# First-layer tables with column-tiled kernels and seven phase buffers, and a reordered feed-forward start and layer-1 projection

## What is computed

```python
# layer 0, attention a: the table. d is the distance, 1024 of them; 64 (batch, head) pairs
phase[h, m*8+w, d] = f1*d/S + f2*sqrt(d)/sqrt(S) + phi        # 3-term product, 16 heads x 128 kernels
feature = sin(2*pi * (phase - round(phase)))
n[b, h, d] = sum_mw gate_weight[b, h, m] * amp[h, m, w] * feature[h, mw, d]
hard = (n > 0); soft = sigmoid(6 * n)                         # straight-through step
bias[b, h, d] = (hard + (soft - hard)) * window[d]
table = (bias, exp(-bias))

# layer 0, mixture: 8 experts, top 2, and one shared expert
x += sum_e w_e(x) * W2_e relu(W1_e ln(x))**2  +  shared

# layer 1, attention a: latent = ln(x) W; q, k, v = latent W_u;
# rotary part r = (latent W_r) * cos + (latent W_r') * sin
```

## Time and profile before

| | us |
|---|---|
| median of 3 runs | 3451.47 |
| lowest and highest | 3448.38, 3469.87 |
| the profiled execution | 3457.46 |
| its span in the profile | 3455.7 |
| mean granted clock of TensorE in it | 0.933 of full |

### The profile page before, as it was taken

How to read it: one execution, slowest core, us unless ns; L and a number is a source line. 1 busy time by engine, 2 the same in 40 slices (tenths; PEclk the granted TensorE clock), 3 DMA queues, 4 the chain that set the end, 5 groups by cost and what they waited for, 6 DMA issues and landing times. The chain is left out here.

```text
span 3455.7 us, 67058 instructions
## 1 busy us (share of the span) xinstructions
PE 3053.0 (88%) x25109; PEld 1677.9 (49%) x25109; DVE 2373.2 (69%) x5084; ACT 1862.5 (54%) x3317; POOL 945.4 (27%) x655
## 2 busy tenths in 40 slices
PE   6778999958599999896799969998999999999899
PEld 3234444423276555573222237764455555555676
DVE  6578888848574554666799942235999999998321
ACT  5336666642264332463599924443666666666444
POOL 1029999971001322000000000001222223232100
PEclk8779999989798999897799969999999999999999
DMA  5212333210330000224322210017434344332000
GB/s 169 71 63 94 106 118 109 91 54 24 104 123 25 1 1 1 99 99 157 106 68 67 62 44 1 1 35 219 112 88 99 98 105 106 97 100 68 12 10 13
DMA packets 215138, 260.69 MB, mean 75 GB/s; under 512 B 45211, under 2 KB 165604, under 8 KB 212497
## 3 DMA queue, kind: packets, MB, share of 16 engines
q1 hardware_dynamic: 214849, 256.83, 25.0%
HBM read 200.72 MB, written 56.55 MB: 74 GB/s over the span
## 5 line engine op out<-in xcount | busy, mean ns | idle before, releaser
L1179 POOL TENSOR_TENSOR l0aa_e<-l0aa_e,l0aa_et 128x1024 f32<-128x1024 f32 (+1 forms) x288 | 512.0, 1816 | 44.6 <-ACT l0aa_e L1322 44.5
L2597 ACT ACTIVATE l1ba_sg<-l1ba_sg,l1ba_mn 128x128 f32<-128x128 f32 (+7 forms) x512 | 394.4, 774 | 185.3 <-DVE l1ba_mn L2649 184.2
L2649 DVE CUSTOM_DVE_ANT_0 l1ba_sg<-l1ba_pS,l1ba_tab 128x128 f32<-128x128 f32 (+7 forms) x512 | 368.0, 743 | 40.9 <-PE l1ba_pS L2538 28.5
L1350 DVE TENSOR_REDUCE l0aa_low<-l0aa_pP 128x8 f32<-128x1024 f32 x288 | 343.2, 1220 | 65.8 <-PE l0aa_pP L1203 61.8
L2659 DVE STREAM_TRANSPOSE l1ba_pT<-l1ba_sg 128x1024 f32<-128x1024 f32 (+3 forms) x344 | 367.1, 1067 | 18.5 <-ACT l1ba_sg L2597 13.5
L319 PEld LDWEIGHTS f_pY<-l_w,f_hT 128*128 128x128 f32 x2048 | 268.8, 192 | 122.9 <-issue 119.5
L2559 PE MATMUL l1ba_pO<-l1ba_pT,l1ba_v 32*64 32x256 f32 x9216 | 320.0, 389 | 7.8 <-ACT l1ba_y L2612 7.8
L3027 ACT ACTIVATE l1aa_e<-l1aa_e 128x1536 f32<-128x1536 f32 x192 | 284.4, 1483 | 33.3 <-DVE l1aa_e L3070 21.0
L282 ACT ACTIVATE f_hT<-f_pH,l_b 128x512 f32<-128x512 f32 x256 | 173.9, 687 | 237.4 <-PE f_pH L311 237.2
L2482 POOL TENSOR_TENSOR l1ba_co<-l1ba_co,l1ba_rb 128x1024 f32<-128x1024 f32 x64 | 151.5, 2367 | 544.3 <-ACT l1ba_co L2605 512.5
L1322 ACT ACTIVATE l0aa_e<-l0aa_pS 128x512 f32<-128x512 f32 x432 | 243.0, 593 | 87.0 <-PE l0aa_pS L1236 48.4
(11 more groups left out here) (407 smaller groups left out, 5103.2 us busy)
## 6 DMA issues: line engine op xcount, KB each, us to landing
f_wB<-l0f_weights SPq DMA_DIRECT2D x16, 2048.0 KB, 7.2
l1ba_rb<-l1b_rdd SPq DMA_DIRECT2D x64, 512.0 KB
l0aa_et<-l0a_table SPq DMA_DIRECT2D x16, 1536.0 KB
l1b_qd<-l1bp_part SPq DMA_DIRECT2D x64, 256.0 KB, 2.4
l1ba_qs<-l1b_qd SPq DMA_DIRECT2D x48, 256.0 KB
l0aa_et<-l0a_table SPq DMA_DIRECT2D x16, 512.0 KB
l1ba_tab<-l1b_table SPq DMA_DIRECT2D x32, 256.0 KB
l1ba_qs<-l1b_qd SPq DMA_DIRECT2D x64, 128.0 KB
```

Of the source, the lines that this page charges most:

```text
L1179: nc.gpsimd.tensor_tensor(es, es, t, ALU.mult).then_inc(multiplied, heads)
L1350: nc.vector.tensor_reduce(low1[:, t, :], pP[TURN[quad, t]][:].rearrange("p (u t) -> p u t", t=P), AX.X, ALU.min).then_inc(p1_low, 1)
L2597: nc.scalar.activation(row, row, ACT.Exp, bias=mn[:, r % 2, i + k:i + k + 1], scale=-1.0, accum_out=den[:, r % 2, i + k:i + k + 1]).then_i ...
L2649: nc.vector.tensor_tensor_reduce(row, scores, bias, 1.0, 3e38, ALU.add, ALU.min, mn[:, r % 2, h:h + 1]).then_inc(m_done, 1)
```

## The change

In `l0a_table`: `fp` and `pos` get 97 rows of zeros (100 rows in all), `win` is loaded on 128 rows. `L` has 32 columns a head, and four heads' products go to four column tiles of the array, result rows 32q to 32q+31 of `pN`; they are issued together by `kernels(k)`, four heads at a time. `fr` has 7 buffers in place of 3, `rn` and `hd` are gone (the rounding writes into `fr`). DVE takes heads 0 to 2 ahead of the gate chain, and PE issues phases 2 to 4 ahead of it. The two DVE operations on `hd` and `sf` become two `scalar_tensor_tensor`, one operation fewer in all. Each of the two tables is stored by four DMAs of 16 rows.

In `l0_ffn`: `ahead` comes behind SP's loop; `f0` loads attention b's weights there, `f1` the weights of layer 1's mixture. `wB` is loaded in four pieces of two experts, each with a semaphore. At the start, the statistics of group 1 come ahead of gate 0, `weights_T(1)` and `to_weT(1)` come in the loop at n = 4, and group 2's transposes and logits come two tiles later than in the other groups.

In `l1a_project`: the norm is cut in two, statistics ahead of the rotary products and Newton steps with apply behind them; `xt` has two buffers; `to_xt` comes ahead of the copy of r on ACT, and the transposes ahead of v on PE.

```diff
@@ l0_ffn
-            if ahead is not None:
-                ahead(sp)
             for g in range(GROUPS):
...
-                sp.dma_start(wB[:, par], we_dram[par:par + 1].broadcast_to([P, E, GROUP])).then_inc(we_in[par], 16)
+                for e in range(0, E, 2):
+                    sp.dma_start(wB[:, par, e:e + 2], we_dram[par:par + 1, e:e + 2].broadcast_to([P, 2, GROUP])).then_inc(we_in[par][e // 2], 16)
+            ahead(sp)
...
-                if e == 0:
-                    dve.wait_ge(we_in[g % 2], 16 * (g // 2 + 1))
+                if e % 2 == 0:
+                    dve.wait_ge(we_in[g % 2][e // 2], 16 * (g // 2 + 1))
...
+            ln_first(lns[0], 0)
+            ln_second(lns[0], 0)
+            ln_first(lns[1], 1)
+            gate_first(gs[0], 0)
+            gate_second(gs[0])
+            gate_weights(gs[0], 0)
+            ln_second(lns[1], 1)
+            gate_first(gs[1], 1)
+            gate_second(gs[1])
+            gate_weights(gs[1], 1)
...
-            weights_T(1)
             for n in range(3, N):
                 g, f = n // HT, n % HT
                 up(n)
+                if n == 4:
+                    weights_T(1)
                 down(n - LAG)
@@ l0a_table
-                     for n, shape in (("fp", [3, 16 * P]), ("pos", [3, SEQ]), ("win", [64, SEQ]), ...
+                     for n, shape in (("fp", [100, 16 * P]), ("pos", [100, SEQ]), ("win", [P, SEQ]), ...
...
-        L = sb("L", [P, H, BH])
-        rn, fr = sb("rn", [P, 2, SEQ]), sb("fr", [P, 3, SEQ])
+        L = sb("L", [P, H, 32])
+        fr = sb("fr", [P, FR, SEQ])
...
-            sp.dma_start(table[1], tb[:]).then_inc(stored, 16)
-            sp.wait_ge(t_ready, 1)
-            sp.dma_start(table[0], te[:]).then_inc(stored, 16)
+            for kind, rows in ((1, tb), (0, te)):
+                if kind == 0:
+                    sp.wait_ge(t_ready, 1)
+                heads = table[kind].rearrange("(b k q) t -> q (b k) t", k=H // COLS, q=COLS)
+                for q in range(COLS):
+                    sp.dma_start(heads[q], rows[32 * q:32 * q + BATCH * H // COLS, :]).then_inc(stored, 16)
...
             def reduce_range(h):
                 dve.wait_ge(u_done, h + 1)
+                if h >= FR:
+                    dve.wait_ge(n_done, (h - FR) // COLS + 1)
+                phase = fr[:, h % FR, :]
+                nc.vector.tensor_scalar(phase, pU[h % 2][:], ROUND, -ROUND, ALU.add, ALU.add).then_inc(f_step, 1)
                 dve.wait_ge(f_step, h + 1)
+                nc.vector.tensor_tensor(phase, pU[h % 2][:], phase, ALU.subtract).then_inc(f_ready, 1)
...
+            def kernels(k):
+                pe.wait_ge(s_ready, COLS * (k + 1))
+                for c in (0, GROUP):
+                    for q in range(COLS):
+                        h = COLS * k + q
+                        ins = nc.tensor.matmul(pN[32 * q:32 * q + 32, c:c + GROUP], L[:, h, :], fr[:, h % FR, c:c + GROUP],
+                                               start=(k == 0), stop=(k == H // COLS - 1), skip_group_check=True)
+                ins.then_inc(n_done, 1)
...
+            for h in range(5, H):
+                phases(h)
+                if h % COLS == 2 and h > COLS:
+                    kernels(h // COLS - 1)
+            kernels(H // COLS - 1)
@@ l1a_project
-                    layernorm(g + 1, 1 - par)
+                    steps = Steps(dve, ln_step, LN_STEPS, g + 1)
+                    ln_statistics(nc, rows(g + 1), S, steps, ln_ve)
                     dve.wait_ge(done["r"], g + 1)
                     nc.vector.tensor_tensor(t1[:], pR[0:R, :], cos[:, t], ALU.mult)
                     nc.vector.tensor_tensor(t2[:], pS[0:R, :], sin[:, t], ALU.mult).then_inc(rope, 1)
+                    normalise(g + 1, 1 - par, steps)
...
+                    to_xt(g + 1, 1 - par)
                     act.wait_ge(r_ready, g + 1)
...
-                    to_xt(g + 1)
...
+                    transposes(g + 1, 1 - par)
                     pe.wait_ge(v_ready, g + 1)
...
-                    transposes(g + 1, 1 - par)
@@ build
-            l0_ffn(nc, D, x, C, "f0", we, ahead=ahead)
+            l0_ffn(nc, D, x, C, "f0", we, lambda sp: load_l0_attn_b(sp, D, C, W))
...
-        l0_ffn(nc, D, x, C, "f1", we)
+        l0_ffn(nc, D, x, C, "f1", we, lambda sp: load_l1_ffn(sp, D, C))
```

More of the change, by code:

```diff
@@ L109, in ln_group_vector, with ln_statistics @@
     return ln_apply(nc, src, out, S)
+def ln_statistics(nc, src, S, steps, ve_ready):
+    for k in range(GROUP_BLOCKS):
+        ins = nc.vector.bn_stats(S["st"][:, k, :], src(k))
+    steps.done(ins)
+    ln_variance(nc, S, steps, ve_ready)
 LN_STEPS = 6
@@ L337, in _, with l0_ffn @@
                 down(n)
-def l0_ffn(nc, D, x, C, tag, we_dram, ahead=None):
+def l0_ffn(nc, D, x, C, tag, we_dram, ahead):
     E = 8
@@ L540, in _ @@
                 g, f = n // HT, n % HT
-                if f == 1 and 1 <= g and g + 1 < GROUPS:
+                if f == (1 if g else 4) and g + 1 < GROUPS:
                     to_weT(g + 1)
@@ L544, in _ @@
                 if g + 2 < GROUPS:
-                    if f == 4:
+                    if f == (4 if g else 6):
                         to_xt(g + 2)
-                    if f == 6:
+                    if f == (6 if g else 7):
                         gate_sigmoid(g + 2)
@@ L609, in _ @@
                 if g + 2 < GROUPS:
-                    if f == 3:
+                    if f == (3 if g else 5):
                         transposes(g + 2)
-                    if f == 5:
+                    if f == (5 if g else 7):
                         logits(g + 2)
@@ L1737, in _ @@
                 act.wait_ge(f_ready, h + 1)
-                nc.scalar.activation(fr[:, h % 3, :], fr[:, h % 3, :], ACT.Sin, scale=TWO_PI).then_inc(s_ready, 1)
-            act.wait_ge(n_done, H)
-            nc.scalar.activation(sf[:], pN[0:BH, :], ACT.Sigmoid, scale=6.0).then_inc(sg_ready, 1)
+                nc.scalar.activation(fr[:, h % FR, :], fr[:, h % FR, :], ACT.Sin, scale=TWO_PI).then_inc(s_ready, 1)
+            act.wait_ge(n_done, H // COLS)
+            nc.scalar.activation(sf[:], pN[:], ACT.Sigmoid, scale=6.0).then_inc(sg_ready, 1)
             act.wait_ge(b_ready, 1)
@@ L1757, in _ @@
             reduce_range(1)
+            reduce_range(2)
             dve.wait_ge(g_in, 32)
@@ L1811, in _ @@
             nc.tensor.matmul(pG[0:BATCH, 0:384], pl[:], gmw[:], start=True, stop=True).then_inc(g_done, 1)
+            phases(2)
+            phases(3)
+            phases(4)
             pe.wait_ge(st, 21)
@@ L1816, in _ @@
             pe.wait_ge(L_ready, 1)
-            for h in range(H):
-                if h + 2 < H:
-                    phases(h + 2)
-                pe.wait_ge(s_ready, h + 1)
-                for c in (0, GROUP):
-                    ins = nc.tensor.matmul(pN[0:BH, c:c + GROUP], L[:, h, :], fr[:, h % 3, c:c + GROUP],
-                                           start=(h == 0), stop=(h == H - 1))
-                ins.then_inc(n_done, 1)
+            for h in range(5, H):
[3 more added lines that the diff above has]
+            kernels(H // COLS - 1)
 def l0a_output(nc, D, x, C, tag, h0, cx, den, out=None):
@@ L3271 @@
         "zeros": np.zeros((64, SEQ), bf16), "ones": np.ones((3, SEQ), bf16), "minus_ones": -np.ones((3, SEQ), bf16),
-        "positions": positions, "window": np.broadcast_to(window, (64, SEQ)),
+        "positions": np.concatenate([positions, np.zeros((97, SEQ), np.float32)]), "window": np.broadcast_to(window, (P, SEQ)),
         "msign": np.repeat(np.float32([-1, 1]), 16).reshape(32, 1),
```

70 lines of the change are left out of this document (30 added, 40 removed).

## The result

The changed kernel took 3412.5 us (median of 4 runs, 3409.5 to 3413.3) beside 3455.7 for the kernel before on the same chip: ratio 0.9868, 95% interval 0.9838 to 0.9897. The forecast was 3407 in a range of 3391 to 3429. A later comparison gave 3421.4 beside 3460.7, ratio 0.9886 (0.9866 to 0.9906); its profile is the last column here. A stage runs from DVE's first operation in it to that of the next; some 109 us lie ahead of the tables' first.

A forecast was written before the change was run, and what follows sets the result against it. Bounds: PE in the tables' head loop, a late gate-weight load in f0, DVE's turns in the projections. Gains 18.5 + 13.3 + 1.3 + 11.1 = 44.2 took 3457.5 to 3413.3, less 6.0 for a median: 3407, range 3391 to 3429.

The forecast's parts named there:

- stalls behind the three blocks: Tables loop: each kernel block between two phases holds DVE up 1.0 us, 3.0 in all (bounds 1.5 and 6).
- cold start: Tables loop: PE idles through the gate chain, so its first two phases run at half clock, 2.2 us (0 to 4).
- The 135 ns for an instruction in column tiles: Tables: 135 ns per column-tile instruction, read from the earlier trace, so 2.2 us for four heads' block of 16.
- the 0.35 of the prediction: Tables: at most 0.35 us a head for both tiling-mode changes and all else; four blocks would cost 1.4.
- weights_T(1) now lies behind it on PE: +0.6: First mixture f0: behind the earlier first product, PE is the bound because of weights_T(1), costing 0.6 us.
- the 1.9 of the forecast: Second mixture f1: the first product comes 1.9 us earlier; less 0.6, the stage gains 1.3 us.
- POOL's wait: Layer-1 projection: DVE's 1.12 us of idling for POOL's power goes, leaving 9.4 us of its own work.
- SP's lag: Layer-1 projection: SP falls behind 0.9 us a group, 3.6 after four; no bound but near, 0.6 at the end.
- it stood 6.0 above the median of the runs, so 3407: Whole kernel: the profiled execution stood 6.0 us above the runs' median, turning 3413.3 into a median of 3407.
- Rival 2: Projections stay near their length, by falling clock or SP's queue: gain 2.7 us instead of 11.1, 3415; chance 0.17.
- rival 3: Tables' kernels: column tiles run one after the other at half clock, 53 us worse, 3460; chance 0.02.
- rival 1: Tables: PE stays at half clock despite padded rows, 14.8 us less gain, 3422; chance 0.13.

The follow-up runs named there:

- run logits: Changed kernel with transposes and logits of group 2 earlier in the first group of f0 and f1: 3413.2 us, ratio 0.9874.
- split_undone: Changed kernel with DVE's layer-norm split undone in the layer-1 projection, PE's and ACT's new order kept: projection 108.3 us, ratio 0.9881.
- rows3: Changed kernel with only the padding taken back, positions and frequencies at 3 rows again: 3440.7 us, ratio 0.9949.
- best: Changed kernel plus earlier logits, padded divisors, and idle products in the tables and at the projection's end: 3407.0 us, ratio 0.9852.
- after_again: The changed kernel itself, unaltered, measured again on the same chip as the kernel with all additions: 3421.4 us, ratio 0.9886.
- pad_alone: Kernel before with only positions and frequencies padded from 3 to 100 rows: 3456.1 us, ratio 0.9991.
- den_pad: Changed kernel with divisor operands in the output projection of layer 1's attention padded from 16 to 100 rows: 3411.0 us, ratio 0.9852.

## Why the prediction held, point by point

*Tables, -18.5 forecast, -21.3 measured.* The mechanism is as told, and all sizes but the stalls were a little too careful. The loop ended at 160.7 instead of 161.8: stalls behind the three blocks 3.4 us (1.28, 1.06, 1.06; forecast 3.0), cold start 1.55 (2.2), a head 2.43 (2.48). The last block took 2.90 (3.3); the tail, from its end to the table's last DVE operation, 4.9 (5.0), and from there the stage's end came 6.6 us later (7.6), where it was 5.6 with two stores. The 135 ns for an instruction in column tiles, taken from the earlier trace rows, was 120 (1.92 / 16). PE reached full clock at 111, as taken. Changes of tiling mode have a small price, which shows from start to start:

```profile
141.71 1.98 PE L1823 MATMUL l0at_pU<-l0a_pos,l0a_fp 100*128 100x512 f32 x4 [0.41 <-DVE l0at_fr L1770]
143.62 1.92 PE L1834 MATMUL l0at_pN<-l0at_fr,l0at_L 128*32 128x512 f32 x16
145.47 3.70 PE L1823 MATMUL l0at_pU<-l0a_pos,l0a_fp 100*128 100x512 f32 x8
```

Four phase instructions without a change take 3.70 - 1.98 = 1.72 us. Four of them and a block, four rounds of four instructions side by side, take 145.47 - 141.71 = 3.76, which is 0.32 more than twice that. So a block costs some 0.3 us for its two changes (an estimate: the rounds are taken to be as long as phase instructions), near the 0.35 of the prediction, and it is part of the stalls. The rule of the Trainium skill ("TensorEngine Tiling (Array Packing)", Key Properties), that a change of mode drains PE, agrees with this trace.

*f0, -13.3 forecast, -13.5 and -11.9 measured.* The first product stands at 24.7 us instead of the 25.7 of the forecast. The step "weights_T(1) now lies behind it on PE: +0.6" was too small: what was late next was the logits of group 2, which gave back some 2 us (run logits). f1 shows it more plainly: its first product moved from 26.7 to 23.0 us, twice the 1.9 of the forecast, and the stage by -1.1 and +0.5.

*Projection, -11.1 forecast, -11.4 and -11.7 measured.* Turns of 9.4 where the clock held and 10.9 where not, mean 9.9 (forecast 10.0). That the sum came out so near is in part luck. The forecast had seven turns shortened by 1.94, 13.6 us, less 1.9 for the first group and 0.6 for the end. Measured were six turns, from a mean of 11.8 to 9.9, 11.4 us; the turn ahead of them grew from 12.5 to 14.2, near the 1.9; and the end, which was to cost 0.6, gave 1.8. The reason was incomplete: I gave POOL's wait the first place, and by run split_undone it is worth 2.6 us of the 11.4, or as little as 0.7 by the spread of this stage. The greater part was the rotary products' own lateness in alternate turns, which rows of 13.34 and 10.54 already showed. SP's lag did no harm.

*The rest, 0 forecast, 2.4 us longer together.* No edit touches these stages, but their code did not take the same time in all profiles. Over the thirteen profiles, and leaving out the two with padded divisors for layer 1, layer 0's attention took 697.9 to 704.4 us, layer 1's 378.2 to 386.3, and the stages behind them 1393.9 to 1403.1, the kernel before having the least. Most of it goes with the time that a stage spends at a granted clock of 0.50, which is twice its length times what its mean granted clock lacks to 1. Layer 1's attention took 378.2 and 378.4 us with 62 to 63 us at half clock, 382.5 and 382.8 with 70 and 74, 383.9 to 384.2 with 77, and 386.2 and 386.3 with 81; so the 5.5 us that it gained here are 63 us at half clock instead of 77, and its first 50 us read 0.83 instead of 0.73. The two values of f0 in the change's order, 164.4 to 164.5 and 165.7 to 166.1, are 22 and 25 us at half clock. What decides when the clock rises stays open.

For layer 0's attention chance is not shown. With the old tables it took 697.9, 701.0 and 701.5 us, with the new ones 699.9 twice (rows3 and best) and 702.2 to 704.4 eight times; time at half clock goes with it here too (89 us in the two, 95 to 104 in the eight), except that the 697.9 had 94. The expectation of run after_again (that stage 698 to 704, rival 704) cannot decide between the two, since it came out at 703.8. In that run the tables and the projection were within 1 us of the first profile as expected, f0 and f1 1.7 and 1.6 us off.

*From the profiled execution to the median.* The sum of 3413.3 for a profiled execution met 3412.6, and that is luck in part: the changed stages gave 3.1 us more than forecast, and the others took back 2.4 that no term had. The step that failed is "it stood 6.0 above the median of the runs, so 3407": three runs were too few for that. With one more the median was 3455.7 and in later comparisons 3459.9 to 3461.5, so the execution had been an ordinary one. Rival 2 did not come, rival 3 neither (120 ns a tile instruction is four side by side); rival 1 is run rows3.

## What to carry to other kernels

Before shrinking a PE stage, ask which of its products keep the clock up: when the work that is taken out is the work with many rows, what remains may run at half clock, and zero rows that cost no PE time give it back; look for busy PE stretches at 0.50 with products of few rows. Judge coupled edits together, since two of these pairs are worth nothing or cost time when only one half is there. And behind each wait removed look up the next one on the same engine, here logits two tiles too late.

## What had not been expected

PE stayed at half clock through 35 us of full work with 3-row products and column tiles of 32 columns, although 48 of the 84 instructions between 134 and 177 us were kernels of 128 rows (three blocks of 3.64 us); in the kernel before, with the same rows but kernels of 64 columns one after the other, it was at full clock. Rows of zeros made a difference: nothing else was added in pad_alone and den_pad, and the clock rose at 106.5 us instead of 133.2 in the one, and to 1.00 where it had stayed at 0.50 in the other. Why is not shown. Sixteen tile instructions take 1.92 us at full clock and 3.64 at half, a quarter of the untiled price at either (7.7 for four heads in pad_alone, and 3.67 for one head at half clock in the kernel before, at 128.9 us). Keeping PE warm with idle products works inside a stage (last block 1.92 instead of 2.90) and was lost over a gap of 2.8 us at a stage's border.
